# A ring of 24 slots for the first layer's fetched rows, filled up to 16 steps ahead, with the maps cleared during routing

## The reference

```python
x = x + linear_then_cumsum(layernorm(x))       # W, bias; cumsum over the 128 columns
x = x + ffn(layernorm(x))                      # mixture of experts, 8 experts, top 2
x = x + local_attention(layernorm(x))          # 16 heads of 8, window of 128
x = x + ffn(layernorm(x))                      # the same weights again
# ffn: xn = layernorm(x)*gamma+beta; p = softmax(xn@router/1.5); two best experts e with weights p_e
#      sum_e p_e * (silu(xn @ W1[e]) @ W2[e]) + x,   W1[e] 128x512, W2[e] 512x128
```

## Time and profile before

| | |
|---|---|
| median of 3 runs | 809.58 us (806.76 to 812.36) |
| profiled execution | 813.83 us, span 812.1 us |
| busy: PE, PEld, DVE, ACT, POOL | 664.5, 516.6, 455.8, 421.8, 331.7 us |
| mean granted PE clock | 0.91 of full speed |
| layer 0 (first fetch to first scores) | 70.70 to 272.26 us |
| attention | 272.26 to 598.74 us |
| layer 1 and the end | 598.74 to 812 us |
| fetches of rows (L502) | 142, mean 980 ns each on POOL |
| gathers back (L522), scatters (L509) | 64 at 962 ns, 71 at 1001 ns |

### The profile page before, as it was taken

The page is one execution under the profiler, slowest core; times in us unless marked ns, Lnnn a source line. Parts: engine busy times, 40 slices in busy tenths (PEclk is TensorE's granted clock), DMA queues, the critical chain, the costliest instruction groups (busy, mean ns, idle before and its releaser), DMA issues.

```text
span 812.1 us, 29237 instructions
## 1 busy us (share of the span) xinstructions
PE 664.5 (82%) x11190; PEld 516.6 (64%) x11190; DVE 455.8 (56%) x1700; ACT 421.8 (52%) x804; POOL 331.7 (41%) x352
## 2 busy tenths in 40 slices
PE   4942988999989788989898988779669799888890
PEld 2521686888878447566665656556448687777680
DVE  7866768522345666575666665573865842224334
ACT  3442375666655047464565657355548465555440
POOL 4303442585777101131212100110056677777771
PEclk9985799999999679899999999797878999999996
DMA  7500031222334301121120201010012111214425
GB/s 225 146 9 17 21 91 44 56 68 73 83 75 116 118 17 60 36 67 50 56 79 20 83 17 58 15 41 6 3 33 73 43 53 51 53 53 116 130 67 165
DMA packets 61029, 52.57 MB, mean 65 GB/s; under 512 B 9729, under 2 KB 54402, under 8 KB 60890
## 3 DMA queue, kind: packets, MB, share of 16 engines
q1 hardware_dynamic: 52034, 32.54, 13.6%
q0 software_dynamic: 8864, 18.17, 8.5%
HBM read 30.74 MB, written 19.92 MB: 62 GB/s over the span
## 4 chain that ended last, share of the span: by engine, by line
PE 47%; DVE 19%; issue 10%; POOL 7%; DMA 7%; ACT 4%; DVEq 4%; SPq 1%; PEld 1%; PEldq 0%; POOLq 0%; ACTq 0%
PE stbank L1208 10%; PE bank L1314 4%; DMA xg<-table,idx 4%; PE stbank L1198 3%; PE sbank L1272 3%; POOL ytab L509 3%; PE sbank L1267 3%; PE stbank L1298 3%; PE stbank L1200 2%; POOL xg L502 2%; DVE mx L889 2%; PE stbank L1199 2%; PE bank L1092 2%; DVE zr L604 2%; PE sbank L1180 1%
## 5 line engine op out<-in xcount | busy, mean ns | idle before, releaser
L502 POOL DMA_INDIRECT xg<-table,idx x142 | 139.1, 980 | 151.0 <-DVE sidx L815 87.5
L1208 PE MATMUL stbank<-wdn,g 128*128 x1136 | 166.6, 291 | 8.9 <-DVE ysb L825 7.6
L1208 PEld LDWEIGHTS stbank<-wdn,g 128*128 128x128 f32 x1136 | 141.6, 196 | 24.5 <-issue 11.7
L889 DVE TENSOR_REDUCE mx<-sbank 128x2 f32<-128x320 f32 (+1 forms) x256 | 116.4, 471 | 72.5 <-PE sbank L1272 67.7
L1033 ACT ACTIVATE pT<-stbank 128x1024 f32<-128x1024 f32 (+1 forms) x128 | 117.0, 916 | 77.0 <-PE stbank L1298 76.5
L973 ACT ACTIVATE xa<-sbank,be_s,ga_s 128x128 f32<-128x128 f32 x142 | 64.9, 457 | 132.2 <-PE sbank L1180 131.4
L1198 PE MATMUL stbank<-xT,wup 128*128 128x128 f16 x568 | 118.5, 229 | 3.9 <-issue 3.7
L1200 PE MATMUL stbank<-xT,wup 128*128 128x128 f16 x568 | 118.7, 229 | 0.0
L1199 PE MATMUL stbank<-xT,wup 128*128 128x128 f16 x568 | 116.7, 225 | 0.0
L522 POOL DMA_INDIRECT cg<-yslot,posi x64 | 61.5, 962 | 128.1 <-ACT pT L1033 114.3
L465 POOL TENSOR_TENSOR r<-ve,mhalf 128x4 f32<-128x4 f32 (+1 forms) x32 | 43.0, 1343 | 157.7 <-DVE ve L584 99.8
(11 more groups left out here) (213 smaller groups left out, 1089.3 us busy)
## 6 DMA issues: line engine op xcount, KB each, us to landing
yslot<-ysb SPq DMA_DIRECT2D x71, 64.0 KB
table<-zr SPq DMA_DIRECT2D x16, 256.0 KB, 2.2
qz<-dumps SPq DMA_DIRECT2D x96, 32.0 KB
kst<-dumps SPq DMA_DIRECT2D x96, 32.0 KB
cg<-ytab SPq DMA_DIRECT2D x12, 256.0 KB, 3.8
xg<-table,idx POOLq DMA_INDIRECT x142
xs<-in_x SPq DMA_DIRECT2D x8, 256.0 KB, 4.8
qz<-in_w SPq DMA_DIRECT2D x1, 2048.0 KB, 9.2
```

Of the source, the lines that this page charges most:

```text
L502: g.indirect_dma_start(xg[:, i % G, :], None, table if t >= FIRST else table[0:CHUNK, :], bass.IndirectOffsetOnAxis(ap=idx[:, t:t + 1], ax ...
L889: ins = v.tensor_reduce(mx[:, qt, 4 * s + 2 * half:4 * s + 2 * half + 2], src, AX.X, ALU.max)
L1208: ins = mm(ybank[i % 2], g32[:, i % 3, P * f:P * f + P], w[:, 0, P * f:P * f + P], start=(f == 0), stop=(f == FC - 1))
```

## The change

The slots for fetched rows move into the memory of `pT`, which attention alone uses, and there are 24 of them instead of 4. In layer 0 the fetches are spread differently over the steps (`fetched_at`): tiles 0 to 3 in step 0, two tiles in each of the steps 1 to 7, tiles 18 to 24 in step 8, and from step 9 on tile s+16. A fetch waits for the transposition of the tile 24 before it. All twelve clearings of `qz` stand in step 8, ahead of its fetches. Layer 1 still fetches tile s+3 in step s, now in the ring of 24; its first fetch also waits until attention's last product with `pT` is done (`s_pv`).

```diff
-G = 4
+G = 24
 RESULTS = 8
-AHEAD = G - 1
-ZERO_AT, ZEROS = 24, 12
+AHEAD, AHEAD_FIRST, SECOND_AT = 3, 16, 8
+ZEROS = 12
...
-        xg = sb("xg", [P, G, D]); xa = sb("xa", [P, 2, P]); xT = sb("xT", [P, 3, 2 * P], F16)
+        xa = sb("xa", [P, 2, P]); xT = sb("xT", [P, 3, 2 * P], F16)
...
         pT = sb("pT", [P, 3, 4 * 256])
+        xg = pT[:].rearrange("p a n -> p (a n)").rearrange("p (g d) -> p g d", d=D)
...
+        def fetched_at(layer, s):
+
+            if layer:
+                return range(AHEAD + 1) if s == 0 else (s + AHEAD,)
+            if s < SECOND_AT:
+                return range(4) if s == 0 else range(2 * s + 2, 2 * s + 4)
+            return range(2 * SECOND_AT + 2, G + 1) if s == SECOND_AT else (s + AHEAD_FIRST,)
...
             def x_step(layer, s):
-                if layer == 0 and ZERO_AT <= s < ZERO_AT + ZEROS:
-
-                    if s == ZERO_AT:
-                        pool.wait_ge(s_wl, E)
+                if layer == 0 and s == SECOND_AT:
+
+                    pool.wait_ge(s_wl, E)
                     n = 3 * NH * SEQ // ZEROS
-                    z = qz[:].rearrange("p u h n -> p (u h n)")[:, n * (s - ZERO_AT):n * (s - ZERO_AT + 1)]
-                    g.memset(z.bitcast(F32), 0.0).then_inc(s_zero, 1)
-                for n in range(AHEAD + 1) if s == 0 else (s + AHEAD,):
+                    for k in range(ZEROS):
+                        z = qz[:].rearrange("p u h n -> p (u h n)")[:, n * k:n * k + n]
+                        g.memset(z.bitcast(F32), 0.0).then_inc(s_zero, 1)
+                for n in fetched_at(layer, s):
                     i, cc, t = layer_tile(layer, n)
                     if i is None:
                         continue
+                    if t == 0:
+                        wait(pool, s_pv, UNITS * B * layer)
                     if t in (0, FIRST):
```

## The result

The changed kernel takes 819.25 us (median of 4 runs, 814.66 to 820.7), the kernel before 809.33 us (median of 4): ratio 1.010, 95% interval 1.005 to 1.015. So it is about 10 us slower, where 3 us less was forecast, and outside the predicted range of 801.5 to 814.5 us. The profiled execution took 820.4 us, its span is 818.7 us.

What follows compares the result with a forecast made beforehand. PE was taken as the bound, with POOL slower from 199.03 us on. Fetching ahead gains 4.7 us and the clearings cost 1.5: 3.2 us less, 810.6 us against the profiled execution, 806.4 against the median; range 801.5 to 814.5 us.

Steps and rivals of the forecast that it cites:

- half a clearing for each of the six: Second chunk's routing: six DVE operations each wait half a clearing, 2.9 us, half on the path: 1.5 us more.
- DVE doesn't get in between clearings at all: Rival at the twelve clearings: DVE stands 10.5 us, 2 covered; 3.8 us more, 813.4 us; chance 0.17.
- own bound of 10.5 us: Upper bound for the clearings in layer 0's routing: DVE held from 112.5 us to the last clearing's end, 123.0 us.
- the held DVE together with a fall of the clock: Case for a time slower than 817.7 us: DVE held at the clearings and an additional clock fall; chance 0.07.
- Fetching ahead: Layer 0, steps 46 to 70: earlier fetches free POOL for the `pow` of steps 58 and 66; 4.7 us less.
- 2.8 + 1.7 = 4.5: At the `pow` of step 58: PE regains 2.8 us of waits and late rows, and 1.7 us without a clock fall.
- PE gets its 0.2 us: At the `pow` of step 66: DVE's 1.92 us wait goes, of which PE gains only 0.2 us.
- The rival of the larger gain: Clearings cost nothing and DVE's time in layer 0 is PE's: 6.9 us less, 802.7 us; chance 0.12.
- The bets on the marks: Wrong if routing's last `pow` to tile 25's fetch grows over 3 us, or fetch to first scores doesn't shrink 3 to 6.
- the two fetches between two `pow`: Steps 1 to 7: one more fetch ahead of each `pow`, 1.25 us; costed at nothing, 1.25 us at most.
- leaving steps 24 to 35: The clearings leave these steps of layer 0, where PE is the bound anyway: no gain.
- layer 1: Fetches stay 3 steps ahead and the new wait for attention's last product ends before the first fetch: nothing.

Runs made afterwards that it cites:

- e2: The kernel before with only the clearings moved, all twelve in a row in step 8, ring and fetches as before: 824.64 us, ratio 1.019.
- e3: The changed kernel with each clearing waiting for the one before it, 0.06 us between two: 803.68 us, 0.992 of the kernel before.
- h5: The kernel before, unchanged, run and profiled once more in an undisturbed set: 808.1 us against 810.0 us, ratio 0.999.
- h6: The changed kernel with clearings one per transposition, and each fetch from tile 26 on also waiting for a transposition: 804.6 us, 0.994 of the kernel before.
- e4: The kernel before with its single clearings in steps 10 to 21 instead of 24 to 35, each right behind a fetch: 815.31 us, ratio 1.008.
- e1: The changed kernel with clearings behind the fetch of tile 24, each after one more transposition: 803.38 us, 0.992 of the kernel before; repeated: 891.0 us, 1.024.
- set 4: One of five groups of runs, each on one chip with the kernel before among them; here the kernel before took 871.8 us.
- disturbed sets: Sets 2 to 4, where the kernel before took 870.6, 866.9 and 871.8 us; in the undisturbed first and last it took 809.5 and 810.0 us.
- f3: The kernel before with single clearings in steps 10 to 21, each waiting for the landing of the fetch ahead: 883.1 us, ratio 1.014, in a disturbed set.
- sets 1 and 2: The first two groups of runs; the kernel before took 809.5 us in the first and 870.6 us in the second.

## Why the prediction was wrong

**The step that failed: "half a clearing for each of the six", 1.5 us.** It measured 13.2 us (e2: 13.4 us alone). The right mechanism stood among the rivals, "DVE doesn't get in between clearings at all", with a chance of 0.17. I put it low for the earlier trace rows, where four `zr` took 0.16 us longer beside two clearings. But those two were 0.31 and 0.20 us long: held to the end of that short row, DVE loses next to nothing in all. The sum of four hid what the first of them shows, and it spoke for the rival:

```profile
15.41 0.70 DVE L604 TENSOR_SCALAR zr<-xs,mv,rr 128x128 f32<-128x128 f32 x1
```

It takes 0.70 us instead of 0.34 us and ends at 16.11 us, 0.08 us behind the end of the second clearing, as all that were held later end just behind their row. The place was off as well: the six operations that the prediction counted from 112.52 us came behind the row, and the `zr` of the sequence before met it. The Trainium skill ("SBUF — State Buffer", Who interferes with whom) says that VectorE in such an operation and GpSimd share a port pair that whoever issues first holds for the whole instruction. Its list of operations fits these runs: `zr` from SBUF waits (11.60 us), the one-hots do not (0.34 and 0.68 us). What it says of the turn is not enough for them: DVE waited not for one instruction of POOL but for all that stood in a row with less than a gap between them.

**Its size was short as well.** The rival gave 10.5 us of hold with 2 covered, 8.5 us. The hold was right: 11.60 - 1.11 = 10.5 us. Nothing of it was covered, and 2.7 us came on top: tile 8 to tile 9 is 11.7 us longer, and tile 9 to tile 10 1.7 us, where the clock of 0.50 reaches to 131.2 us (tile 9 is at 127.6 us, tile 10 at 132.3 us). With a low clock at these two tiles some 3 us more pass there without any row (see e3), so it is enough for the 1.7 us; that it is all of them isn't shown.

**The range.** With the hold uncovered, the prediction's own bound of 10.5 us would have given 809.6 + 10.5 - 4.7 = 815.4 us, over the 814.5 us at which its range ended. For more than 817.7 us it had named the held DVE together with a fall of the clock, at 0.07, and that is what came. And for less than 801.5 us it gave 0.16, more than the 0.12 of the only rival that leads there.

**Fetching ahead: mechanism right, size 7.2 us instead of 4.7.** The `pow` of step 58 ran 0.54 us after POOL began to wait for DVE, as forecast, the first addition waits 1.87 us (2.8 forecast), and the low clock near 234 us is gone. By the terms: up to tile 66 the change gains 1.0 + 3.9 = 4.9 us, where 2.8 + 1.7 = 4.5 were forecast; but h5 has no low clock there and is 0.3 us slower on the whole way, so the 1.7 us was the wrong name for a part of the waits. From tile 66 to 70 it gains 2.3 us where I had "PE gets its 0.2 us". That was the mis-sized term. I took PE's one wait for DVE's copy at 255.17 us as all that DVE's 1.92 us cost, but a copy into `xT` is late by it too and PE's transpositions stood 3.4 and 2.6 us apart there. The rival of the larger gain had this right ("DVE's time is PE's", 6.9 us); that its sum comes near 7.2 us is in part luck, for it holds the same 1.7 us. That both rivals held at once, one on each side, stood in no case of mine.

**The bets on the marks.** The last `pow` of the routing to the fetch of tile 25 grew from 41.3 to 54.5 us, and the fetch of tile 25 to the first scores shrank from 119.8 to 111.8 us counted to the first product of scores (the prediction's 119.6 us count to the mask's product just ahead of it), 8.0 us instead of 3 to 6. What was costed at nothing was nothing: the two fetches between two `pow` (38.2 us from the first fetch to tile 8 in the changed kernel and h6, 38.1 us before; other profiles go up to 39.2 us with one fetch there and to 40.8 us with two), leaving steps 24 to 35 (e4), and layer 1.

**From the stretches to the medians.** 13.2 - 7.2 = 6.0 us, and the spans differ by 6.6 us, while the medians differ by 9.9 us. The profiled execution of before was one of the slower of its kind (813.83 us, median 809.33), that of the change an ordinary one. Where it was slow is seen beside h5: 342.1 us against 334.0 us between tile 70 and layer 1, and within 0.3 us of it in the stretches from the first fetch on. By medians the halves add up better: e2 gives 15.1 us more and e1 6.2 us less, 8.9 us together. e1 and e3, with the row's hold gone, are 6.2 and 5.9 us under before, which is what is left when only the 7.2 us stay. **They are the versions that beat both kernels**: 0.992 with intervals below 1, and h6 0.994; but in set 4 e1 took 1.024 of before.

**What stays open.** What makes PE and DVE issue slowly in the disturbed sets. That the hole goes with a run of fetches is shown by its place in seven kernels and its absence in f3; that the run causes it was not tested on its own, since h6 did not break the run, and the undisturbed sets have longer runs without a hole. Why layer 1 is 30 to 37 us longer in disturbed sets is as open. Why there are sets of both kinds is unknown; sets 1 and 2 ran on the same chip. How far ahead a fetch must be, and what the ring alone is worth in an undisturbed set, wasn't measured.

## What to carry to other kernels

Ask for each operation that you put beside another engine not only how long it is, but how many of its kind follow each other without a gap: here VectorE, when it had to wait, got its turn at the end of the row, so a semaphore wait between two GpSimd fills, 0.06 us each, was worth 10 us here from tile 8 to tile 21. The sum over a short overlap in the trace of before says nothing of a long one: look at the single instruction, and at what its end coincides with. And a wait of the engine that feeds the bound can be worth its whole length, as the 1.92 us of DVE here, and not only the wait that the bound shows right behind it.

## What the runs showed of the hardware

- Twelve MEMSETs of 128x1024 f32 in a row on POOL take 10.76 us and hold a `tensor_scalar` from SBUF to SBUF on DVE for 10.5 us; with 0.06 us between them, 12.13 us, and the four `zr` take 1.78 us. Rows of three hold it until the third has ended (118.25 us, `zr` to 118.34 us), and a single one until it has ended (155.89 us, a `tensor_scalar` of 128x46 from 154.99 to 155.93 us instead of 0.19 us).
- An indirect DMA's issue with a MEMSET right behind it is a row, too, and by itself it is not (the four `zr` of the earlier trace rows take 1.11 us beside one): `zr` 113.00 to 114.75 us, fetch to 113.70, clearing to 114.67.
- Two-input operations of DVE beside the same block are undisturbed: 0.34 and 0.68 us.
- Tile 8 to tile 10 takes 7.3 us at a granted clock of 1.00 in ten profiles, and 10.3 to 10.6 us in four where it is 0.50 for about 10 us from tile 8 on.
- The same kernel, e1, took 803.4 us in one set and 891.0 us in another. In the second, PE issued 15 matmuls in 23 us and DVE 2 operations while POOL issued 19 fetches, in the first 241 and 23. Layer 1 took 214.0 us in the first set and 247.3 us in the second.
